# Half of the expert rows summed in DRAM by indirect DMA instead of by one-hot matmuls

## The reference

```python
    buf = jnp.zeros((E, CAP + 1, H), x.dtype).at[se, slot].set(x[tok])[:, :CAP]
    h = jax.nn.silu(jnp.einsum('ech,ehf->ecf', buf, w_gate)) * jnp.einsum('ech,ehf->ecf', buf, w_up)
    out = jnp.einsum('ecf,efh->ech', h, w_down)
    gathered = out[se, jnp.minimum(pos, CAP - 1)] * valid.astype(x.dtype)[:, None]
    w = topk_w.reshape(-1)[order].astype(x.dtype)[:, None]
    return jax.ops.segment_sum(gathered * w, tok, num_segments=Tn)
```

## Time and profile before

| | |
|---|---|
| median of 3 executions | 452.96 us (451.02 to 453.14) |
| profiled execution: time, span | 450.25 us, 448.4 us |
| TensorE busy | 397.3 us (89%) |
| VectorE busy | 357.7 us (80%) |
| ScalarE busy | 218.3 us (49%) |
| GpSimd busy | 105.1 us (23%) |
| granted TensorE clock, mean | 0.960 |

### The profile page before, as it was taken

The page is one execution under the profiler, slowest core; times in us unless marked ns, Lnnn a source line. Parts: engine busy times, 40 slices in busy tenths (PEclk is TensorE's granted clock), DMA queues, the critical chain, the costliest instruction groups (busy, mean ns, idle before and its releaser), DMA issues.

```text
span 448.4 us, 5081 instructions
## 1 busy us (share of the span) xinstructions
PE 397.3 (89%) x1664; PEld 214.9 (48%) x1664; DVE 357.7 (80%) x659; ACT 218.3 (49%) x406; POOL 105.1 (23%) x76
## 2 busy tenths in 40 slices
PE   0988999989993997989999999999999899997673
PEld 0433464676841465766776773444444344432221
DVE  4999979899699479898979879527977966559995
ACT  3774655681295275647765583521111141157770
POOL 1000004200000521232330000147684754440000
PEclk9999779999998598999999999999999999999897
DMA  7940000640078418875676530540000000000011
GB/s 259 401 181 1 2 0 0 238 174 1 0 244 273 101 45 233 233 248 179 204 191 212 219 117 1 205 170 1 0 1 0 1 0 0 1 0 0 1 48 47
DMA packets 12251, 47.45 MB, mean 106 GB/s; under 512 B 2897, under 2 KB 5434, under 8 KB 9794
## 3 DMA queue, kind: packets, MB, share of 16 engines
q1 hardware_dynamic: 11074, 43.20, 27.4%
q0 software_dynamic: 1152, 3.93, 3.9%
HBM read 44.76 MB, written 2.37 MB: 105 GB/s over the span
## 4 chain that ended last, share of the span: by engine, by line
PE 48%; DVE 27%; issue 14%; POOL 4%; DMA 3%; ACT 2%; SPq 0%; POOLq 0%; DVEq 0%
PE bank L1718 7%; PE bank L1705 6%; PE bank L1582 4%; POOL arena L389 4%; PE bank L1750 3%; PE bank L1747 3%; PE bank L1447 3%; PE bank L1400 2%; DMA arena<-token_rows,arena 2%; PE bank L1673 2%; PE bank L1498 2%; PE bank L1357 2%; DMA kT<-in_kT 2%; PE bank L1770 1%; PE bank L1611 1%
## 5 line engine op out<-in xcount | busy, mean ns | idle before, releaser
L686 ACT ACTIVATE early<-bank 128x512 f32<-128x512 f32 (+1 forms) x24 | 14.3, 597 | 86.0 <-PE bank L1718 76.6
L1582 PE MATMUL bank<-onehot,rows 128*128 128x512 f32 x192 | 51.8, 409 | 0.0
L1246 DVE TENSOR_TENSOR early<-early,bank 128x512 f32<-128x512 f32 (+1 forms) x24 | 16.4, 684 | 37.8 <-ACT early L686 33.3
L1718 PE MATMUL bank<-arena 128*128 128x512 f32 (+1 forms) x96 | 42.2, 600 | 0.1
L389 POOL DMA_INDIRECT arena<-token_rows,arena x24 | 27.5, 1145 | 58.6 <-PE bank L1620 52.7
L1582 PEld LDWEIGHTS bank<-onehot,rows 128*128 128x128 f32 x192 | 34.4, 191 | 10.3 <-issue 3.9
L1705 PE MATMUL bank<-cT,arena 128*128 128x512 f32 x80 | 37.9, 596 | 0.0
L400 POOL TENSOR_TENSOR early<-early,arena 128x512 f32<-128x512 f32 (+1 forms) x12 | 20.1, 1672 | 62.6 <-DMA arena<-pair_weights 55.7
L406 POOL TENSOR_TENSOR early<-early,arena 128x512 f32<-128x512 f32 x10 | 22.3, 2228 | 29.3 <-DVE early L1246 29.3
L1718 PEld LDWEIGHTS bank<-arena 128*128 128x128 f32 (+1 forms) x96 | 15.7, 181 | 22.6 <-issue 21.2
L1065 DVE TENSOR_SCALAR onehot<-const,arena 128x1024 fp32r<-128x1024 f32 x24 | 18.0, 752 | 9.7 <-PE bank L1582 9.2
(11 more groups left out here) (371 smaller groups left out, 872.3 us busy)
## 6 DMA issues: line engine op xcount, KB each, us to landing
arena<-in_w_gateup SPq DMA_DIRECT2D x16, 768.0 KB, 6.3
arena<-in_w_down SPq DMA_DIRECT2D x8, 768.0 KB, 10.4
arena<-in_wq SPq DMA_DIRECT2D x1, 2048.0 KB
arena<-in_wo SPq DMA_DIRECT2D x1, 2048.0 KB, 7.9
const<-in_const SPq DMA_DIRECT2D x1, 1688.0 KB, 11.3
arena<-in_w_upgate SPq DMA_DIRECT2D x1, 1408.0 KB, 5.8
kT<-in_kT SPq DMA_DIRECT2D x2, 512.0 KB, 5.4
xT<-in_xT SPq DMA_DIRECT2D x1, 1024.0 KB, 9.0
```

Of the source, the lines that this page charges most:

```text
L1582: return mm(bank[2 * ct + ch][:], rows1[:, i % RRING, part, ct * P:(ct + 1) * P], onehot1[:, t, ch * CHUNK:(ch + 1) * CHUNK], start=False, ...
L1718: last = mm(dst, (bup, bga)[z][:, f * P:f * P + fw], ((zu1, zg1), (zud, zgd))[k][z][:, ch * CHUNK:(ch + 1) * CHUNK], start=False, stop=Tru ...
```

## The change

Two of the three tiles (t = 0 and 2) of groups 0 to 5 are called `ADDED`, the 12 others `PLACED`. `PLACED` tiles go as before. For `ADDED` tiles there is no rounded part, no one-hot, no remainder and no scatter matmul. GpSimd adds their 128 rows of 1 KB by an indirect DMA with accumulation to a table in DRAM, `expert_sums`. It holds three sets of 1024 token rows (plus spare rows for empty slots), chosen by the expert, so that no row occurs twice in one DMA. Each add waits until the one before has landed.

The sets are zeroed near the start by a GpSimd fill and three DMAs of 128 x 9216 B. At the end GpSimd reads the three sets back into `accs`, 1 MB each, the second and third accumulating, each after the one before has landed. 16 TensorE products of 128 x 128 with the identity add them to the banks, just before the last tile's scatter. VectorE works out the row numbers in five small operations.

The output buffers of t = 0 and 2 are doubled (`outbuf`). In groups with added tiles ScalarE evicts in the order 1, 0, 2. The gathers of group g + 3 now stand in GpSimd's queue between the two adds of group g. SyncE issues the gate and up weights of a group as soon as gate and up of the group two before is done; the down weights have a semaphore of their own and are issued at the old moment. Several semaphores are merged, which does not change what waits for what.

```diff
+ADDED = [(g, t) for g in range(6) for t in (0, 2)]
+PLACED = [(g, t) for g in range(NG) for t in range(GT) if (g, t) not in ADDED]
+NACC, ACCROWS = 3, 16
...
+            step(g.memset(zeros, 0.0))
             pool.wait_ge(S("for_pool"), 1)
...
+            for a in range(NACC):
+                g.dma_start(sums[a * P * ACCROWS:(a + 1) * P * ACCROWS, :].rearrange("(p r) c -> p (r c)", r=ACCROWS)[:, 0:(NT + 1) * C],
+                            zeros).then_inc(S("acc_added"), 16)
+            pool.wait_ge(S("acc_added"), 16 * NACC)
...
             def experts(g):
                 if g >= 2:
-                    sp.wait_ge(S("ffn1_done"), g - 1)
+                    sp.wait_ge(S("gu1_done"), 2 * (g - 1))
...
-                sp.dma_start(r["d"], I["w_down1"][:, e, :]).then_inc(S(f"ring{g % 2}_in"), 16)
+                if g >= 2:
+                    sp.wait_ge(S("ffn1_done"), g - 1)
+                sp.dma_start(r["d"], I["w_down1"][:, e, :]).then_inc(S(f"ringd{g % 2}_in"), 16)
...
-            for t in range(ST):
-                if t % GT == 0 and t >= 2 * GT:
-                    pool.wait_ge(S("h1_turned"), 2 * (t // GT - 1))
...
+            def add_rows(g1, t):
+                n, i = ADDED.index((g1, t)), g1 * GT + t
+                pool.wait_ge(S("outw_ready"), out_count(g1, t))
+                pool.wait_ge(S("acc_added"), 16 * (NACC + n))
+                g.indirect_dma_start(sums[:, :], bass.IndirectOffsetOnAxis(ap=tokacc[:, i:i + 1].bitcast(U32), axis=0),
+                                     outbuf(g1, t), None, compute_op=ALU.add).then_inc(S("acc_added"), 16)
+
+            gathers(0)
+            gathers(1)
+            pool.wait_ge(S("h1_turned"), 2)
+            gathers(2)
+            for g1 in range(NG):
+                if (g1, 0) in ADDED:
+                    add_rows(g1, 0)
+                if g1 + 3 < NG:
+                    gathers(g1 + 3)
+                if (g1, 2) in ADDED:
+                    add_rows(g1, 2)
+            for a in range(NACC):
+                pool.wait_ge(S("acc_added"), 16 * (NACC + len(ADDED) + a))
+                g.dma_start(accs.rearrange("p t c -> p (t c)"),
+                            sums[a * P * ACCROWS:(a + 1) * P * ACCROWS, :].rearrange("(p r) c -> p (r c)", r=ACCROWS)[:, 0:NT * C],
+                            accum_op=ALU.add if a else ALU.bypass).then_inc(S("acc_added"), 16)
...
-                    if g >= 1:
-                        act.wait_ge(S("rows1_ready"), i - GT + 1)
-                    if i >= RRING:
-                        act.wait_ge(S("scat1_done"), i - RRING + 1)
+                    before = (g - 1 if t == 1 else g - 2, t)
+                    if before in ADDED:
+                        act.wait_ge(S("acc_added"), 16 * (NACC + ADDED.index(before) + 1))
+                    elif before in PLACED:
+                        act.wait_ge(S("rows1_ready"), PLACED.index(before) + 1)
...
+            rowbits, rest = tokacc.bitcast(U32), tokbits.bitcast(U32)
+            v.tensor_scalar(rowbits, tokf, float(N), spare, ALU.is_ge, ALU.mult)
+            dve.wait_ge(S("toki_ready"), 1)
+            step(v.tensor_scalar(rest, toki.bitcast(U32), P - 1, 4, ALU.bitwise_and, ALU.logical_shift_left))
...
+            def sums_to_banks(ct):
+                pe.wait_ge(S("acc_added"), 16 * (len(ADDED) + 2 * NACC))
+                for t in range(NT):
+                    mm(bank[2 * ct + t // 4][:, t % 4 * P:(t % 4 + 1) * P], accs[:, t, ct * P:(ct + 1) * P], ident,
+                       start=False, stop=False, skip_group_check=True)
...
-                for k in range(first, first + n):
-                    t, ct, part, ch = k // 8, k // 4 % 2, k // 2 % 2, k % 2
+                tiles = [t for t in range(GT) if (g, t) in PLACED]
+                for k in range(first, min(first + n, 8 * len(tiles))):
+                    t, ct, part, ch = tiles[k // 8], k // 4 % 2, k // 2 % 2, k % 2
...
             for ct in range(CT):
                 for t in range(GT):
+                    if t == GT - 1:
+                        sums_to_banks(ct)
                     last = scatter(NG - 1, t, ct)
```

More of the change, by code:

```diff
@@ L82 @@
 K_PL = K_EM + ST * E1
-K_W = K_PL + 2 * GE
+K_ACC = K_PL + 2 * GE
+K_W = K_ACC + GT + 1
 V_W, V_U, V_WR, V_LN1, V_LN2 = 0, 8, 16, 18, 20
@@ L130, in build @@
         scratch = nc.dram_tensor("token_rows", [N + 1, ROW], F32, kind="Internal").ap()
+        sums = nc.dram_tensor("expert_sums", [NACC * P * ACCROWS, C], F32, kind="Internal").ap()
         pair_weights = nc.dram_tensor("pair_weights", [2, N], F32, kind="Internal").ap()
@@ L206, in build @@
         ws1, wr1 = at(o, NT), at(o + 8, NT); o += 16
-        tokf, toki, wslot = at(o, ST), at(o + ST, ST), at(o + 2 * ST, ST); o += 3 * ST
+        tokf, toki, wslot, tokacc, tokbits = (at(o + ST * i, ST) for i in range(5)); o += 5 * ST
         assert o <= AC, o
@@ L260, in l2bufs, with outbuf, out_order, out_count @@
             return lbuf[0], lbuf[1], lbuf[3 + (it % 2)], lbuf[2], lbuf[5 + (it % 2)], lbuf[7]
+        def outbuf(g, t):
+            return outw2[:, t // 2, :] if t != 1 and g % 2 else outw[:, t, :]
+        def out_order(g):
+            return (1, 0, 2) if (g, 0) in ADDED else (0, 1, 2)
+        def out_count(g, t):
+            return GT * g + out_order(g).index(t) + 1
         def tail2(it):
@@ L382, in _, with gathers @@
             pool.wait_ge(S("rows_out"), 48)
-            for t in range(ST):
-                if t % GT == 0 and t >= 2 * GT:
-                    pool.wait_ge(S("h1_turned"), 2 * (t // GT - 1))
[L386 to L391, removed]
+            def gathers(g1):
+                for t in range(g1 * GT, (g1 + 1) * GT):
+                    if t >= XRING:
+                        pool.wait_ge(S("xgT_done"), (t - XRING) // GT + 1)
+                        pool.wait_ge(S("wslot_ready"), (t - XRING) // GT + 1)
+                    g.indirect_dma_start(xg[:, t % XRING, :], None, scratch[:, :],
+                                         bass.IndirectOffsetOnAxis(ap=toki[:, t:t + 1].bitcast(U32), axis=0)
+                                         ).then_inc(S(f"gather{g1 % 4}"), 16)
@@ L638, in _ @@
                     scaled(3, 1)
-                for t in range(GT):
+                for t in out_order(g):
                     i = g * GT + t
@@ L826, in _ @@
                 last = v.tensor_copy(wbat[:, ct, ::B + 1], vecs[:, V_WR + ct:V_WR + ct + 1].to_broadcast([P, B]))
-            last.then_inc(S("wbat_ready"), 1)
+            last.then_inc(S("place0_ready"), 1)
             for ct in range(CT):
@@ L1121, in _ @@
                 for t in range(GT - 1):
-                    slot_onehot(g, t)
+                    if (g, t) in PLACED:
+                        slot_onehot(g, t)
                 for t in range(GT):
-                    slot_rest(g, t)
+                    if (g, t) in PLACED:
+                        slot_rest(g, t)
                 if g == 0:
@@ L1558, in _ @@
                           start=True, stop=True)
-            last.then_inc(S("slotT_done"), 1)
+            last.then_inc(S("counts1_done"), 1)
             def shared_down(ct, ch):
@@ L1577, in scatter_one @@
             def scatter_one(g, t, ct, part, ch):
[L1579 to L1583, removed]
+                n = PLACED.index((g, t))
+                pe.wait_ge(S("onehot1_ready"), n + 1)
+                pe.wait_ge(S("rows1_ready"), n + 1)
+                return mm(bank[2 * ct + ch][:], rows1[:, n % RRING, part, ct * P:(ct + 1) * P],
+                          onehot1[:, n % GT, ch * CHUNK:(ch + 1) * CHUNK], start=False, stop=((g, t) == PLACED[-1] and part == 1))
+            def sums_to_banks(ct):
[3 more added lines that the diff above has]
+                       start=False, stop=False, skip_group_check=True)
             def scatter_run(g, first, n):
-                for k in range(first, first + n):
-                    t, ct, part, ch = k // 8, k // 4 % 2, k // 2 % 2, k % 2
+                tiles = [t for t in range(GT) if (g, t) in PLACED]
+                for k in range(first, min(first + n, 8 * len(tiles))):
+                    t, ct, part, ch = tiles[k // 8], k // 4 % 2, k // 2 % 2, k % 2
                     last = scatter_one(g, t, ct, part, ch)
@@ L1625, in down @@
                 r = ring[g % 2]
+                pe.wait_ge(S(f"ringd{g % 2}_in"), 16 * (g // 2 + 1))
                 if g < NG - 1:
@@ L1824, in _ @@
             base2(1, 0)
-            pe.wait_ge(S("mtb_ready"), 1)
+            pe.wait_ge(S("oh2_ready"), 2)
             pe.wait_ge(S("z2_read"), 2)
@@ L1897, in constants @@
     k[:, K_PL:K_PL + GE] = (p[:, None] % GE == np.arange(GE))
-    k[:, K_PL + GE:] = (p[:, None] % E1 // GE == np.arange(GE))
+    k[:, K_PL + GE:K_ACC] = (p[:, None] % E1 // GE == np.arange(GE))
+    expert = slot[0:GT].T // CAP
+    k[:, K_ACC + GT] = ACCROWS * p
+    k[:, K_ACC:K_ACC + GT] = (expert % 5 % NACC * P * ACCROWS).astype(np.uint32).view(np.float32)
     return k
```

54 lines of the change are left out of this document (32 added, 22 removed).

## The result

The changed kernel takes 476.85 us (median of 4, 473.94 to 479.57), the one before 452.79. The ratio is 1.054, its 95% interval 1.050 to 1.058. The profiled execution has a span of 472.0 us at a mean clock of 0.925. The forecast was 448.4 with a range up to 459: wrong in sign and outside the range.

A forecast was written before the change was run, and what follows sets the result against it. TensorE bounds the kernel; after the change the add chain and read-back do. First add 169.2, 11.5 us periods, adds landed 237.3, sums in SBUF 255.3, stage end 262.6 instead of 267.1: gain 4.5, so 448.4 us; range 438 to 459.

The forecast's parts named there:

- the adds are slow: Rival, expert stage: kernel ends slower than before once L passes 6.5; at L = 7.5 a loss of 5; chance 0.18.
- five periods from first add to first add: GpSimd's queue, groups 0 to 5: a period of 11.5 us each, putting the first add of group 5 at 226.9.
- last two adds: End of the add chain, no gathers between and few weights beside: 5.0 each with 0.2 each, 10.4 us.
- read-back: Three 1 MB transfers of the sums into SBUF in series, two accumulating: 16.1 to 21.2 us, 18.0 taken.
- L: Landing time of a group's second add, priced from gathers of 128 rows: 5.6 us, with ends 3.5 and 8.5.
- L = 8.5: Slow end of the landing; with the last two adds as slow and accumulating reads at 7.9: 287, a loss of 20 us.
- The rule on the receipt: Rival on DRAM adds: last-write receipt makes each add land 1 us later than a gather; loss of 2.5; chance 0.10.
- the other estimate: Read-back by the skill page, 2.0 us plus bytes at 436 GB/s: 4.4 us each, 13.2 in all.
- The products: TensorE, behind the wait for the sums: 16 small products that bring the sums in, about 1.8 us.
- The pace without the chain: Groups 1 to 5 of the expert stage: VectorE's in-order queue sets the pace at 10.2 us a group.
- the free zeroing: Near the kernel's start: zeroing the sums writes 3.5 MB beside the first loads, 8.6 us, and costs nothing.
- my first rival: The queue keeps pace: L at most 4.2, adds follow outputs at 10.2 us; gain of 14, 439; chance 0.23.

The follow-up runs named there:

- four tables: Changed kernel with a DRAM table per output buffer, so no add waits for the last one; only the first table zeroed and read back: 447.66 us, ratio 0.992.

## Why the prediction was wrong

The path of the forecast was right: the chain of adds in GpSimd's queue, then the read-back, sets the end. Its case put TensorE's waits for gathers at nothing, and there were 15.9 us of them; the run with the gathers in front shows that only 4.2 us of the total hang on these. I had put the case "the adds are slow", with gathers late in mid-stage, at 0.18; that case came. The sum's own steps, with what they measured:

| step | forecast | measured | difference |
|---|---|---|---|
| first add starts | 169.2 | 168.2 | -1.0 |
| five periods from first add to first add | 57.7 | 76.8 | +19.1 |
| last two adds | 10.4 | 12.8 | +2.4 |
| read-back | 18.0 | 24.0 | +6.0 |
| clock and work behind the wait | 7.3 | 8.9 | +1.6 |
| end of the stage | 262.6 | 290.8 | +28.2 |

The step that failed is the period, 5.95 + L = 11.5, of which 15.4 were measured. Its two halves were both short.

From the first add to the second I had 5.75 us, and it took 7.2 on average (10.5, 6.6, 5.8, 7.2, 5.8). I had priced the issue as a gather's 0.95; an add takes 1.6 to 2.1. And I had called the first add's landing hidden by the gathers. In group 0 it landed 9.7 us after issue, 3.9 us after the gathers were out.

From the second add to the next first one I had L = 5.6 and 0.2 to wake; it took 8.2, a landing of 7.4 and 0.8. I had mixed the loaded and the quiet gathers two to one, but the adds ran while the engines were 0.93 to 0.95 busy in groups 1 and 2, where the quiet rows no longer apply. I had added nothing for reading and adding at the target, on a DRAM write of 2.6 us without accumulation; the run with plain writes puts the accumulation at 1.3 us a link, GpSimd's issue included. The bound L = 8.5 was in the text, but the formula at the measured 7.4 gives 271.7, not 290.8: the leg from the first add to the second was 5.75 in every rival, and the read-back and the last two adds were moved only in the extreme of L = 8.5, which gave 287.

**The rule on the receipt** (the Trainium skill, DMA: Bandwidth & Descriptors, Anatomy of one DMA): plain indirect writes to DRAM still made links of 6.1 us, so the trace does not refute it. It does not bear it out either: a link holds issues, queueing and transfer too, and what share is the receipt no run shows.

**The read-back.** 16.1 to 21.2 us was the span that I gave it; it took 24.0 to 26.6. Alone an accumulating 1 MB took 8.2 us, above my upper 7.9 (a plain one took 5.3, beside my 5.35; none came down to the 4.4 of the other estimate), and the traffic of the next stage's weights, which I had named only in a rival, is in every run.

**The products.** I counted 16; they are 32 matmuls in the trace, since each product in this format runs as two. The six turns whose 0.87 us I took as the price show as one matmul each. At full clock they cost 3.4 us (one half: 288.05 to 289.76), not 1.8, and the run with read-back only has the same 3.4 in its trace.

**What held.** The pace without the chain: 10.2 us a group was forecast, 9.9 was measured with four tables. The 8.7 us of TensorE for a group, the free zeroing (the run with zeroing and read-back costs no more than its products) and the start of the adds held as well. So did the 1.2 GHz clock behind the long wait. The first half of the products ran at a granted clock of 0.52, near that level, and took 3.31 us; the second half ran at full clock and took 1.71:

```profile
281.89:285.20 3.31, 3.31 (x17) 3.31 (x17) 0.00 (x0) 0.00 (x0) 0.00 (x0) 0.52 0.00 0
...
288.05:289.76 1.71, 1.71 (x18) 1.71 (x16) 1.11 (x2) 0.38 (x1) 0.00 (x0) 1.00 0.00 0
```

With the adds out of series the time is below that of the kernel before, as in my first rival (439 there, 447.7 here, with a 26.6 us read-back and twice the products), though that run leaves three quarters of the sums out.

## What to carry to other kernels

Before moving work to a DMA that adds in place, count the links: n transfers that must wait for one another cost n times the issue, the loaded landing, the wake and what else stands between them in the queue, here 7.5 us each, and every later order in the same queue stands behind them. Leaving the weight loads out took 20 us off the time, in a single execution, and taking the adds out of the series took 29. Take the loaded landing for every link once the change itself fills the transfers, and use only as many links as the pace of the producing engine hides: against the same kernel without adds, five here gained 0.9%, six nothing, and twelve lost some 6%. Move also the bad values of all terms together in a rival: here the landings, the gathers and the read-back were all long beside the same weight loads.

## What the runs showed of the hardware

An indirect DMA of 128 rows of 1 KB that adds kept GpSimd for 1.6 to 2.1 us in the changed kernel (3.0 at most with four tables), a plain indirect write for 1.0 to 1.9, mostly under 1.3, a gather for 0.95 at its shortest. The adding one moved as 128 packets of 1 KB, the plain one as 32 of 4 KB: the changed kernel shows 14842 packets, the one with plain writes 13690, with the same 55.70 MB. Adds landed after 3.7 to 9.7 us in the changed kernel, 6.2 at the median. With the 16 DMA engines 0.99 busy over 57 us, gathers and weights still kept TensorE supplied. A 1 MB transfer that accumulates into SBUF took 8.2 us with nothing beside it, a plain one 5.3 with some traffic beside it.
